# Attention on one core: two heads' scores per pass through the PE array, paired maxima, and an order worked out from costs

## The reference

```python
def _L1_attn_ref(x, Wqkv, bqkv, Wo, bo):      # x: 1 x 1024 x 256, h = 16 heads, d = 16
    qkv = x @ Wqkv + bqkv
    q, k, v = (heads(z) for z in jnp.split(qkv, 3, axis=-1))
    att = jnp.einsum('bhqd,bhkd->bhqk', q, k) / math.sqrt(c)
    att = jnp.where(tril, att, -jnp.inf)
    att = jax.nn.softmax(att, axis=-1)
    out = jnp.einsum('bhqk,bhkd->bhqd', att, v)
    return out.transpose(0, 2, 1, 3).reshape(b, t, c) @ Wo + bo
```

## Time and profile before

| | us |
|---|---|
| median of 3 runs | 662.7 (661.95 to 669.58) |
| profiled execution | 666.22 |
| its span, first to last instruction | 664.6 |
| of it, first mixture of experts | about 257 |
| layer norm, projections, stacking | 257 to 297.5 |
| attention: scores, softmax, values, `Wo` | 297.5 to 506.7 |
| second mixture of experts | 506.7 to 664.6 |

### The profile page before, as it was taken

How to read it: one execution, slowest core, us unless ns; L and a number is a source line. 1 busy time by engine, 2 the same in 40 slices (tenths; PEclk the granted TensorE clock), 3 DMA queues, 4 the chain that set the end, 5 groups by cost and what they waited for, 6 DMA issues and landing times.

```text
span 664.6 us, 11232 instructions
## 1 busy us (share of the span) xinstructions
PE 540.9 (81%) x3784; PEld 433.1 (65%) x3785; DVE 425.4 (64%) x1121; ACT 286.6 (43%) x649; POOL 169.7 (26%) x175
## 2 busy tenths in 40 slices
PE   1649999999999980579999899899987269899940
PEld 1649999999999970456655455555555268889840
DVE  4748888888877732649876467587225657787620
ACT  2323544445445321260155345464743037667630
POOL 6031304314312204630000100100000045576631
PEclk9859999999999995698599879999998569899985
DMA  8633555555564106053000400400001335576721
GB/s 322 186 122 121 177 158 144 157 178 144 147 187 120 19 8 177 0 112 79 1 1 1 96 1 1 95 2 1 1 0 64 99 87 120 153 162 173 155 33 16
DMA packets 46541, 63.48 MB, mean 96 GB/s; under 512 B 5440, under 2 KB 34624, under 8 KB 46464
## 3 DMA queue, kind: packets, MB, share of 16 engines
q1 hardware_dynamic: 36112, 47.80, 23.3%
q0 software_dynamic: 10368, 14.89, 13.0%
HBM read 45.84 MB, written 11.60 MB: 86 GB/s over the span
## 4 chain that ended last, share of the span: by engine, by line
PE 68%; DVE 13%; issue 6%; DMA 5%; ACT 3%; POOL 1%; POOLq 1%; DVEq 1%; ACTq 0%; SPq 0%
PE banks L645 22%; PE banks L694 10%; PE banks L909 8%; PE banks L883 7%; PE banks L927 6%; PE banks L698 5%; PE banks L678 2%; PE banks L651 2%; DMA got<-rows,from_row 2%; DVE w_lo L1222 2%; DMA rows<-rows 2%; DVE maxes L1467 2%; PE banks L912 1%; PE banks L887 1%; ACT gated_y L1037 1%
## 5 line engine op out<-in xcount | busy, mean ns | idle before, releaser
L1111 ACT ACTIVATE probs<-banks 128x512 f32<-128x512 f32 (+3 forms) x192 | 88.7, 491 | 105.1 <-PE banks L912 82.6
L1467 DVE TENSOR_REDUCE maxes<-banks 128x1 f32<-128x512 f32 (+1 forms) x192 | 97.3, 553 | 35.7 <-PE banks L887 23.8
L1222 DVE TENSOR_TENSOR w_lo<-stage,w_hi 128x512 fp32r<-128x512 f32 (+1 forms) x200 | 90.8, 505 | 21.3 <-ACT w_hi L981 20.5
L557 POOL DMA_INDIRECT got<-rows,from_row x50 | 52.4, 1049 | 162.0 <-DMA rows<-rows 128.9
L883 PE MATMUL banks<-k_st,q_st 96*128 96x512 f32 (+1 forms) x192 | 80.2, 455 | 7.8 <-issue 6.5
L645 PE MATMUL banks<-xg_hi,w_hi 128*128 128x320 f32 (+2 forms) x328 | 82.5, 333 | 4.5 <-DVE xg_lo L1350 2.2
L981 ACT ACTIVATE w_hi<-stage 128x512 fp32r<-128x512 f32 (+1 forms) x200 | 83.6, 485 | 0.5 <-DMA stage<-in_w 0.5
L694 PE MATMUL banks<-w_hi,a_hi 128*128 128x256 f32 (+1 forms) x296 | 78.7, 295 | 3.1 <-DVE a_hi L1320 1.8
L909 PE MATMUL banks<-q_st,k_st 128*128 128x512 f32 (+2 forms) x192 | 79.6, 438 | 1.6 <-DVE q_st L1485 1.3
L645 PE MATMUL banks<-xg_lo,w_hi 128*128 128x320 f32 (+2 forms) x328 | 78.0, 320 | 0.0
L645 PE MATMUL banks<-xg_hi,w_lo 128*128 128x320 f32 (+2 forms) x328 | 77.9, 319 | 0.0
(11 more groups left out here) (193 smaller groups left out, 816.6 us busy)
## 6 DMA issues: line engine op xcount, KB each, us to landing
stage<-in_w SPq DMA_DIRECT2D x48, 512.0 KB, 5.8
stage<-in_ffn_w SPq DMA_DIRECT2D x36, 256.0 KB, 3.7
rows<-rows SPq DMA_DIRECT2D x2, 1056.0 KB, 5.4
q_st<-qk_hi SPq DMA_DIRECT2D x16, 128.0 KB, 2.6
xT<-in_xT SPq DMA_DIRECT2D x2, 512.0 KB, 4.4
tok<-res SPq DMA_DIRECT2D x2, 512.0 KB, 4.4
k_st<-qk_hi POOLq DMA_DIRECT2D x16, 64.0 KB, 4.4
k_st<-qk_hi SPq DMA_DIRECT2D x16, 64.0 KB, 2.9
```

The source lines that it names most:

```text
L557: pool.indirect_dma_start(got[:, par, t, :], None, rows_d, bass.IndirectOffsetOnAxis(from_row[:, par, t:t + 1], 0)).then_inc(s[f"gathered{ ...
L1111: act.activation(probs[:, (s % 2) * HG + j, c0:HALF], bank[3 + n % TURN_BANKS][:, c0:HALF], ACT.Exp, scale=float(C) ** -0.5).then_inc(by_s ...
L1222: ins = dve.tensor_tensor(lo, src, f32(hi), ALU.subtract)
L1467: dve.tensor_reduce(maxes[:, g % 2, j, i:i + 1, c], out[:, 0:w], AX_X, ALU.max).then_inc(by_vector, 1)
```

## The change

- **Stacks.** A head's three parts of q take 48 rows, two heads of a pair stand at rows 0 and 64, and the same for k, so no zeros and no second version of k. K is 48 for `rows`, 50 for `cols` (two rows for the maxima; ones in `k_st`). Three stacks instead of two; 24 DMAs a group, 12 on SP (q), 12 on POOL (k), all of 16 partitions x 4 KB.
- **Scores.** Each `rows` and `cols` piece now issues two matmuls, one per head, in the two 64-row halves of the array. `rows` puts them in the two banks of a slot (two slots of two banks), and DVE takes both maxima in one reduction over 2 x width. `cols` uses three banks in turn.
- **Masks.** In `rows` two f32r matmuls of 256 columns with an f32r identity, over all 128 rows. In `cols` none: POOL zeroes the upper triangle of the four heads' exponentials with one select per diagonal step (32 in all), and PE waits for it before `values`.
- **Maxima.** By unit (group and half of the queries), one `maxrow` a unit: transposed to 8 rows, copied to `max_rows`, then four DMAs on SP into `q_st`.
- `take` moves from DVE to ACT. Value sums use one bank. `probs` gets a third set.
- **Order.** `attention_order` computes the list greedily, from costs written into it for PE, DVE and ACT, with a 0.3 us preference for `cols`. In the list that comes out, rows run up to two units ahead of the columns; the loads of group 3 (`stack3`) stand after unit 1's last values, and unit 7's columns (the last) have only `wo` pieces beside them.

The diff, cut to its core:

```diff
+STEPS = [[kt for kt in range(QT * (qb + 1))] for qb in range(NH)]
+UNITS = [(g, qb) for g in range(GROUPS) for qb in range(NH)]
+TURN_SLOTS = 2
+EXP_BANKS = 3
+PROB_SETS = 3
+STACKS = 3
+HASTE = 0.3
...
+    stack_at = {0: 13.0, 1: 18.0, 2: 24.0}
+    while rows or cols or waiting or after:
...
+        start, _, kind = min(picks)
+        start += HASTE if kind == "cols" else 0.0
+        if kind == "rows":
+            u, pr, i, c = rows.pop(0)
+            g, qb = UNITS[u]
+            w = min(HALF, (i + 1) * P - c * HALF)
+            on_vector(("rows", u, pr, i, c), stack_at[g], (0.35 if c == qb else 0.1) + max(w, 2 * P) / 2400,
+                      0.2 + 2 * w / 960)
...
+            if piece[0] == "maxrow":
+                done = on_vector(piece, at, 0.5, 0.7)
+                order.append(("maxdma", u))
+                max_at[u] = done + 3.0
...
-TURN_BANKS = 3
-STACKED = 2 * D
-MAX_ROW = 3 * STACKED
+TERMS = 3 * D
+WITH_MAX = TERMS + 2
...
-    q_st = in_slots("q_st", [P, 2, 2, T], F32R)
-    k_st = in_slots("k_st", [P, 2, 2, 2, T], F32R)
+    q_st = in_slots("q_st", [P, STACKS, 2, T], F32R)
+    k_st = in_slots("k_st", [P, STACKS, 2, T], F32R)
...
     def stack_part(eng, g, pr, c, qk, h):
...
+        dst = slice(P // 2 * h + D * c, P // 2 * h + D * (c + 1))
+        to = (q_st, k_st)[qk][dst, g % STACKS, pr, :]
...
-        for g in range(GROUPS):
-            stack_free(sp, g)
+        for piece in ORDER:
+            if piece[0] == "stack":
+                g = piece[1]
+                stack_free(sp, g)
+                for pr in range(2):
+                    for c in range(3):
+                        for h in range(2):
+                            stack_part(sp, g, pr, c, 0, h).then_inc(stacked_q[g % STACKS], 16)
+            elif piece[0] == "maxdma":
...
+                sp.wait_ge(by_vector, BY_VECTOR["maxrow", u] + 1)
+                for pr in range(2):
+                    for h in range(2):
...
+                        sp.dma_start(q_st[at_row:at_row + 2, g % STACKS, pr, qb * HALF:(qb + 1) * HALF].bitcast(F32),
+                                     max_rows[first:first + 2, u % 2, :]).then_inc(max_in[u % 2], 16)
...
-        pool.memset(k_st[:, 0].bitcast(F32), 0.0).then_inc(k_zeros, 1)
-        pool.memset(k_st[:, 1].bitcast(F32), 0.0).then_inc(cleared, 1)
-        pool.memset(max_t[:, :, :, :], 0.0).then_inc(cleared, 1)
+        for h in range(2):
+            half = k_st[P // 2 * h + P // 4:P // 2 * (h + 1)].rearrange("p a b t -> p (a b) t")
+            link(pool.memset(half.bitcast(F32), 1.0))
...
+            elif piece[0] == "values" and piece[1:] in DIAGONAL:
...
+                pool.wait_ge(by_scalar, BY_SCALAR["cols", u, step, HG - 1] + 1)
+                tri = probs_of(u, step)[:, :, c0:c0 + P]
+                pool.affine_select(out=tri, in_=tri, compare_op=ALU.is_ge, fill=0.0, base=0,
+                                   pattern=[[0, HG], [1, P]], channel_multiplier=-1).then_inc(causal, 1)
...
+        def row_scores(u, pr, i, h, out, c):
...
+            return pe.matmul(out[:, 0:w], q_st[lo:lo + TERMS, g % STACKS, pr, i * P:(i + 1) * P],
+                             k_st[lo:lo + TERMS, g % STACKS, pr, c * HALF:c * HALF + w], start=True, stop=True)
+
+        def row_mask(i, out):
+
+            d = (i % QT) * P
+            first, cols = (0, mask_r[:, P:3 * P]) if d == 0 else (d - P, mask_r[:, 0:2 * P])
+            return pe.matmul(out[:, first:first + 2 * P], ident_r[:, :], cols, start=False, stop=True,
+                             skip_group_check=True)
...
+                pe.wait_ge(stacked_q[g % STACKS], 16 * 12 * (g // STACKS + 1))
+                pe.wait_ge(stacked_k[g % STACKS], 16 * 12 * (g // STACKS + 1))
...
+                for h in range(2):
+                    mm = row_scores(u, pr, i, h, out[:, h * HALF:(h + 1) * HALF], c)
+                if c == qb:
+                    for h in range(2):
+                        mm = row_mask(i, out[:, h * HALF:(h + 1) * HALF])
                 mm.then_inc(to_vector, 1)
...
+                pe.wait_ge(max_in[u % 2], 16 * 4 * (u // 2 + 1))
...
+                for h in range(2):
+                    n = BY_SCALAR["cols", u, step, 2 * pr + h]
+                    if n >= EXP_BANKS:
+                        pe.wait_ge(by_scalar, n - EXP_BANKS + 1)
+                    lo = P // 2 * h
+                    pe.matmul(exp_bank[n % EXP_BANKS][:, c1:HALF],
+                              k_st[lo:lo + WITH_MAX, g % STACKS, pr, kt * P:(kt + 1) * P],
+                              q_st[lo:lo + WITH_MAX, g % STACKS, pr, qb * HALF + c1:(qb + 1) * HALF],
+                              start=True, stop=True).then_inc(to_scalar, 1)
...
+                if (u, step) in DIAGONAL:
+                    pe.wait_ge(causal, DIAGONAL[u, step] + 1)
...
+            elif kind == "take":
+                u = piece[1]
+                act.wait_ge(pv_done, PVS[u, len(STEPS[UNITS[u][1]]) - 1] + 1)
+                if u >= 2:
+                    act.wait_ge(by_vector, BY_VECTOR["out", u - 2] + 1)
+                act.activation(taken[:, u % 2, :], bank[7][:, :], ACT.Copy).then_inc(taken_out, 1)
...
+                dve.tensor_reduce(maxes[:, u % 2, 2 * pr:2 * pr + 2, i % QT, c],
+                                  out[:, :].rearrange("p (h t) -> p h t", h=2)[:, :, 0:w], AX_X, ALU.max
                                   ).then_inc(by_vector, 1)
```

420 lines of the change are left out of this document (230 added, 190 removed).

## The result

| | before | after |
|---|---|---|
| median, us (4 runs each, side by side) | 666.14 (661.95 to 670.85) | 681.74 (681.09 to 683.03) |
| ratio | | 1.0235, 95% interval [1.0146, 1.0323] |
| span of the profiled execution | 664.6 | 680.7 |
| mean granted clock, whole span | 0.889 | 0.851 |

What follows compares the result with a forecast made beforehand. PE was taken to bound the attention, its sum falling from 181 to 130 us. Start to 321.5, middle 117 us and end put the stage's end at 473.6 instead of 506.7: gain 33 us from 662.7, 630 us, range 603 to 656.

Steps and rivals of the forecast that it cites:

- The end of unit 7 and the tail: After unit 7's max rows at 438.5: DMA 5 us, exponentials 17 us to 460.5, tail 12.1 plus 1 to 473.6.
- PE's work in the middle: From the first exponential (321.5) to unit 7's max rows (438.5): 100 us of PE left, within 117 us together.
- 4 us for half clock: Added to the middle because PE's clock had been at half early in the attention and again from 377 to 391.
- Rival 4: PE's clock stays at half for the whole middle, work 1.5 times as long: 677 to 680 us; chance 0.06.
- my fixed 0.10 us of the score: Each 512-column score on PE: 0.32 us taken as 0.213 of streaming plus a fixed 0.10.
- Rival 3's drain: Each of some 180 shape changes on PE waits for a whole pipeline, 0.25 to 0.29 us: 660 us; rival 3's chance 0.15.
- my 0.07: Masked rows piece on PE: the last 0.07 us in 0.147 + 0.10 + 0.24 + 0.07 = 0.56.
- every pair as one stream: PE's scores: two heads in the two halves cost one stream plus 0.10 us; bounds 0.5 and 1.0 of present streaming per head.
- the sign that the halves do not run at once: In the profile after: two matmuls of a pair 0.2 us or more apart would point to rival 3, chance 0.15.
- the factor of 1.10 for the coupling: Middle: PE's 100 us stretched to 110 because three engines are close and maxima arrive through DMA; bounds 1.00 and 1.20.
- my 2 us for the memsets: Start: two memsets of k_st, 5.3 us each, end later and slow the rows normalisations on the chain: +2 us.
- The 36 issues on SP's queue: Start: unit 0's max DMAs stand behind three stacks' loads until 315.5, putting the first exponential near 321.5.

Runs made afterwards that it cites:

- the replanned list: Order computed from measured costs, against the kernel with whole 64-row masks that keep the shape and a mended start: 651.18 us, ratio 0.9809 to before.

## Why the prediction was wrong

**Right.** PE bounds, before and after. The two halves can run at once (a pair whose banks are both free takes as long as one). The select takes 635 ns (I took 0.7), reductions 425, 690, 957, 1224 ns (0.42 to 1.22), the `take` 603 ns. The loads of the maxima hold nothing: PE waited for them for 2 us in all. The end of unit 7 and the tail were off by 6 us together.

**The step that failed** is PE's work in the middle: the forecast took 100 us at full clock and 4 more for the half clock. After, PE was busy 144 us there, 66 us of the stretch at half clock.

**Wrong, the clock.** I took 4 us for half clock, since before came back to full by itself. After had 66 us of it in the middle. At the 0.30 to 0.43 us each of the runs with K = 48 and K = 128, that is an estimated 20 to 28 us, 16 to 24 more than I took: the larger part of the miss. Rival 4 named this place and priced it at 1.5 times the work, but I gave it 0.06 because I tied the clock to PE waiting. The runs show that waiting isn't what sets it: with both heads in the lower half PE was busy 199 of 203 us and at half clock throughout. That rival 4's 677 to 680 us lie next to the measured 681.7 is partly luck: it had half clock over the whole middle, and it covered 44%.

**Wrong, the price of a change of shape.** I read 0.14 us, there and back, from a values step, and took 0.17 for the masks. What I had read was the way out of the values step alone (0.35 for 0.213 in after as well, 0.14). The way in was hidden in my fixed 0.10 us of the score ahead of it. Measured it is 0.21 to 0.23 on the way in and to and from a mask, 0.30 at half clock. In the middle: 54 masked pieces x 0.09 to 0.19 = 5 to 10 us, 40 values steps x 0.12 = 5: an estimated 10 to 15 us of PE that I did not have. The timelines show the price. What it came to in the kernel's time no run isolates: leaving the masks out gave 18 us, which is no more than I had charged for them, while half clock rose by 14; the masks in the same half gave 16, of which 7 to 10 are streaming at once. The Trainium skill (TensorEngine Tiling, Key Properties) speaks against this change, as the prediction said, and I weighed it with a row that did not hold the whole trip. Rival 3's drain, 0.25 to 0.29 a change, was nearer to what came than my 0.07.

**Wrong, every pair as one stream.** The `cols` pairs that wait for a second bank (above) cost 5.5 us in the middle. The forecast named matmuls 0.2 us or more apart as the sign that the halves do not run at once; a fifth of the `cols` pairs showed it for another reason, the three banks.

The parts fit the whole: of PE's 144 us, 20 to 28 are the clock's, which leaves 116 to 124 against 100; the shape and the split pairs make 15 to 20 of that difference. Clock, shape and split pairs together are 31 to 45 us, where the middle was 35 longer and the factor of 1.10 for the coupling already held 10. That factor no run isolates, and the replanned list moved the time by an amount that its interval does not resolve.

**Wrong, the start.** It came 6 us late. The loads began 1.6 us later than before, which my 2 us for the memsets cover. But PE waited for all 24 of them, and the last, issued at 296.91, landed 6.4 us later: the wait cost 4 us where I had 2, and the first rows came 2 us late. Then rows pieces took 1.2 to 1.5 us each at half clock with their masks, where I had 0.82. The 36 issues on SP's queue, which I had as the limit, ended at 313.97; the maxima were ready only at 322.9. I had the wait at the wrong engine. In the run of the start alone, taking this wait and one memset away moves the first exponential by 10.6 us.

**What stays open.** What sets the granted clock in the halves; how the 35 us split between shape, clock and split pairs (shape and clock multiply, a change costs 0.30 instead of 0.21 at half); what a fourth bank toward ACT would give, which no run tried; and whether a list exists in which the halves keep the full clock.

## What to carry to other kernels

Price a change of the array's shape by the way in and the way out, each from its own pair of start times in the trace, before splitting a matmul into halves; and keep what goes with it, a mask above all, in the same shape, even if it takes a trick (here it turned 0.64 to 0.77 us into 0.26). If two matmuls are to run at once, have their outputs come free together: the rows pairs, with two banks a slot, were split 3 times in 96, the `cols` pairs, with three banks in turn, 21 times. Doubling what runs at once need not pay on an engine whose clock is granted: ask what the granted clock will be in the new form, and try one kernel with the same columns in whole-array matmuls before building on halves. An order with fewer changes of shape is not better by itself, if it holds buffers longer.

## What the runs showed of the hardware

- The same 1028 PE instructions with the same columns ran at a granted clock of 0.97 with K = 128 and 0.53 with K = 48 in the lower half, 193 against 316 us, though PE was busy in 98% of the slower stretch. Zeros in the extra rows did not hinder that.
- Two matmuls in the two 64-row halves, f32r, 512 columns: 0.50 us for both, 0.50 for one. Filling both halves with zeros to 64 rows left half clock at 102 us against 101 (and 84 against 97 in another list).
- A change between half-array, whole-array and 32-column tiles: 0.21 to 0.23 us at full clock, 0.14 out of the values step, 0.30 at half. About half of it falls behind the change: two 256-column masks take 0.43 us from the first to the next pair after a change, 0.24 in the whole-array run without one. At a change the weight load starts with its matmul, without one 0.1 to 0.2 us ahead of it. No change: 0.12 to 0.22 us from one pair of 256 columns to the next.
- GpSimd's memset slows DVE's normalisation beside it: eight took 7.82 us while the second of two memsets of 32 partitions ran (10.53 us together), 3.06 where one over 128 partitions (5.22 us) was just ending, and 2.67 with nothing beside. The memset's time did not go by partitions: 5.2 to 5.3 us for 6144 elements in each of 32 or of 128.
